# First attention scores in four row groups and four PSUM banks, tiles 10 and 11 of the FFN turned by TensorE, in a new order of work

## What is computed

```python
# 1: attention on 64 latent keys, the best 4 kept per head (16 heads of 16 columns)
Q = x @ Wq.T + bq;  V = x @ Wv.T + bv
logits = einsum('bhtd,lhd->bhtl', Q, latent) / 4
w = softmax(top_4(logits));  y = (w @ latent + V) @ Wo.T + bo
x = layernorm(x + y)
# 2: attention on 64 rows of a context (rope applied), 16 heads, folded weights
scores = q_r @ k_r.T;  ctx = softmax(scores) @ kv_rope;  x = layernorm(x + (ctx @ w_kc_kv) @ Wo.T)
# 3: FFN with ternary weights and activations rounded to 8 bits
linear_bit(x, w, g) = round_to_127(g * rmsnorm(x)) @ ternary(w).T
h = silu(linear_bit(x, w1, g1)) * linear_bit(x, w2, g2)
x = layernorm(x + linear_bit(h, w3, g3))
```

## Time and profile before

| | |
|---|---|
| median of 3 runs | 341.52 us |
| the profiled execution: its time | 342.95 us |
| its span, first to last instruction | 341.2 us |
| mean granted TensorE clock | 0.986 |
| transfers | 22.28 MB, of them 15.01 MB read from HBM |

### The profile page before, as it was taken

How to read it: one execution, slowest core, us unless ns; L and a number is a source line. 1 busy time by engine, 2 the same in 40 slices (tenths; PEclk the granted TensorE clock), 3 DMA queues, 4 the chain that set the end, 5 groups by cost and what they waited for, 6 DMA issues and landing times.

```text
span 341.2 us, 6916 instructions
## 1 busy us (share of the span) xinstructions
PE 322.0 (94%) x2245; PEld 232.6 (68%) x2264; DVE 285.6 (84%) x718; ACT 281.7 (83%) x535; POOL 249.9 (73%) x234
## 2 busy tenths in 40 slices
PE   8899999998899999999999999999999999989892
PEld 4677777766667677767777866776768767666341
DVE  2475489999499999998989999898999998798882
ACT  2476888984768778989899789899999898998883
POOL 3274757799297798989958697989489686577661
PEclk9699999999999999999999999999999999999998
DMA  7989830000000002011021102130401222210001
GB/s 214 422 325 386 281 140 0 2 1 3 0 2 1 17 1 46 2 38 41 1 46 37 28 4 46 32 63 1 48 17 32 62 35 52 55 33 16 13 22 46
DMA packets 24852, 22.28 MB, mean 65 GB/s; under 512 B 19824, under 2 KB 22256, under 8 KB 23920
## 3 DMA queue, kind: packets, MB, share of 16 engines
q1 hardware_dynamic: 24816, 21.84, 21.6%
...
HBM read 15.01 MB, written 2.10 MB: 50 GB/s over the span
## 4 chain that ended last, share of the span: by engine, by line
PE 44%; DVE 24%; issue 12%; POOL 9%; ACT 8%; DMA 2%; SPq 0%; POOLq 0%; DVEq 0%; ACTq 0%
PE small L585 6%; PE wide L550 5%; PE wide L471 3%; PE wide L483 3%; PE wide L534 3%; PE small L458 3%; DVE m L1105 3%; PE small L635 3%; DMA region_r<-in_wqkr 2%; DVE r L1170 2%; PE wide L564 2%; PE wide L609 2%; DVE ch L1236 2%; DVE m L1157 2%; PE small L506 2%
## 5 line engine op out<-in xcount | busy, mean ns | idle before, releaser
L585 PE MATMUL small<-V_sb,PT_sb 128*128 128x256 f32 x256 | 58.1, 380 | 0.3
L585 PEld LDWEIGHTS small<-V_sb,PT_sb 128*128 128x128 f32 x256 | 47.9, 190 | 8.4 <-issue 1.2
L1375 POOL TENSOR_TENSOR Ls<-Ls,m 128x1024 f32<-128x1024 f32 x16 | 31.5, 1967 | 26.1 <-DVE mask L1119 26.1
L550 PE MATMUL wide<-B_sb,x1T 128*128 128x512 f32 x192 | 49.4, 406 | 1.1 <-ACT PT_sb L866 1.0
L550 PEld LDWEIGHTS wide<-B_sb,x1T 128*128 128x128 f32 x192 | 35.2, 188 | 13.0 <-ACT PT_sb L866 2.7
L1440 POOL TENSOR_TENSOR region_c<-region_c,region_q 128x1024 f32<-128x1024 f32 (+1 forms) x17 | 32.6, 1919 | 14.5 <-DVE region_c L1229 12.0
L1105 DVE MAX8 m<-Ls 128x8 f32<-128x64 f32 x256 | 33.9, 210 | 8.9 <-ACT Ls L796 8.7
L1390 POOL TENSOR_TENSOR Ls<-Ls,mask 128x1024 f32<-128x1024 f32 x16 | 38.8, 2427 | 2.4 <-ACT Ls L809 1.8
L1413 POOL TENSOR_TENSOR P<-P,r 128x1024 f32<-128x1024 f32 x16 | 34.0, 2125 | 4.5 <-DVE r L1173 4.5
L1382 POOL TENSOR_TENSOR mask<-mask,r 128x1024 f32<-128x1024 f32 x16 | 30.4, 1902 | 8.4 <-DVE r L1128 8.4
L609 PE MATMUL wide<-tern,region_k 128*128 128x512 bf16 x111 | 28.1, 379 | 1.7 <-issue 0.6
...
## 6 DMA issues: line engine op xcount, KB each, us to landing
region_q<-in_wqx SPq DMA_DIRECT2D x1, 2048.0 KB, 17.3
region_c<-in_woTx SPq DMA_DIRECT2D x1, 2048.0 KB, 7.7
...
region_c<-in_wkcqT SPq DMA_DIRECT2D x1, 1536.0 KB, 11.8
...
```

Of the source, the lines that this page charges most:

```text
L550: mm = pe.matmul(ps_L2[:, r * 512:(r + 1) * 512], x1T[:, u, k, :], B_sb[:, s, w, k, r * 512:(r + 1) * 512], start=(u == w == k == 0), stop ...
L585: mm = pe.matmul(ps_O2[:, 0:D], PT2_sb[:, c, :], V_sb[:, c, :], start=(c == 0), stop=(c == PAIRS - 1))
L1375: pool.tensor_tensor(heads(Ls[n % 2][:]), heads(Ls[n % 2][:]), over_heads(m8[:, :, 0:1]), ALU.subtract).then_inc(g_d1, 1)
```

## The change

`L1` is cut finer: 8 products instead of 4 for a tile, each with 32 rows (2 heads) of weights and 128 columns of result, in four row groups that write four banks. These are half of each bank of `wide[1]` and `wide[2]`, so `L1` now waits for both and takes both. `lat_k` has two heads side by side instead of four and is made by one reduction and 2 products instead of 4. `copy_L1` still has two instructions of 512 columns, each now reads from the two banks of one wide tile. `TURNED` goes from 12 to 10: tiles 10 and 11 are turned by TensorE too. Several other steps move to other PSUM tiles, and the order of work is written anew on all engines.

```diff
-TURNED = 12
+TURNED = 10
-        lat_k = sb("lat_k", [P, KD, 4 * L])
+        lat_k = sb("lat_k", [P, KD, 2 * L])
+        odd_even = sb("odd_even", [P, 2])
-        ps_L1 = wide[1]
-        ps_XQT = small[1]
-        ps_HT = small[0]
+        ps_XQT = small[0]
+        ps_HT = wide[0]
-        ps_T2T = wide[2]
+        ps_T2T = wide[1]
-        ps_V = (wide[2], wide[2])
-        ps_T1 = (wide[2], wide[0])
-        ps_A = (wide[1], wide[2])
+        ps_V = (wide[2], wide[1])
+        ps_T1 = (wide[0], wide[1])
+        ps_A = (wide[0], wide[0])
-        ps_Z_last = (wide[0], wide[1])
-        ps_HT_last = (wide[0], wide[2])
+        ps_L1 = (wide[1], wide[2])
+        ps_Z_last = (wide[1], wide[2])
+        ps_HT_last = (wide[1], wide[0])
             def L1(n, *freed):
-                bank_of(*freed)
+                for k in range(0, len(freed), 2):
+                    bank_of(*freed[k:k + 2])
                 for g in range(KD):
-                    for j in range(2):
-                        mm = pe.matmul(ps_L1[:, j * 512 + g * SEQ:j * 512 + (g + 1) * SEQ],
-                                       QT[b % QRING][j * L:(j + 1) * L, g, q * P:(q + 1) * P],
-                                       lat_k[j * L:(j + 1) * L, g, :], start=True, stop=True)
+                    for j in range(4):
+                        rows = slice(32 * j, 32 * (j + 1))
+                        col = (j % 2) * 512 + g * 2 * L
+                        mm = pe.matmul(ps_L1[j // 2][:, col:col + 2 * L],
+                                       QT[b % QRING][rows, g, q * P:(q + 1) * P], lat_k[rows, g, :],
+                                       start=True, stop=True)
-            warm(9, wide[0]); Q(0); warm(4, wide[0], p_warm, 1); L1(0); T1_(0)
-            T1_(1, p_warm, 2); L1(1, a_L1, 1); Q(1, a_Q, 1); T2_(a_T1, 2); L1(2, a_L1, 2)
+            warm(9, wide[0]); Q(0); warm(4, wide[0], p_warm, 1); L1(0)
+            warm(5, wide[0], p_warm, 2); L1(1, a_L1, 1, a_L1, 1); T1_(0, p_warm, 3)
+            T1_(1, a_L1, 2); Q(1, a_Q, 1); T2_(a_T1, 1); WF(a_Q, 2); T2T(a_T1, 2)
...
             def copy_L1(n):
-                for j in range(2):
+                for half in range(2):
                     ins = act.activation(
-                        Ls[n % 2][:].rearrange("p (g j n) -> p j g n", g=KD, j=2)[:, j],
-                        ps_L1[:, j * 512:(j + 1) * 512].rearrange("p (g n) -> p g n", g=KD), ACT.Copy)
+                        Ls[n % 2][:].rearrange("p (g h j n) -> p h g j n", g=KD, h=2, j=2)[:, half],
+                        ps_L1[half][:].rearrange("p (j y g n) -> p y g j n", j=2, y=2, g=KD)[:, 0], ACT.Copy)
...
+                link(dve.tensor_reduce(odd_even[:], head_rows[:].rearrange("p e (j i) -> p i e j", i=2),
+                                       mybir.AxisListType.XY, ALU.add))
...
             def sum_2(n):
                 dve.wait_ge(a_ex2, n + 1)
+                since(dve, v_sm2, n)
```

More of the change, by code:

```diff
@@ new lines, in _ @@
+            A_(1, a_PT1, 2); WT(1, v_y1, 1); L1(3, v_bl, 1, a_C, 1); Q(3, a_Q, 3)
+            PT1(2, a_A, 2); B_(1, 0, a_L1, 4); B_(2, 0, a_L1, 4); B_(3, 0, a_PT1, 3)
+            O1(1, a_AT, 2); X1T(0, a_Q, 4); L1(4, v_bl, 3, v_bl, 2); WT(2, v_y1, 2)
+            L2(0, v_bl, 4); O1(2, a_AT, 3); X1T(1, v_xlo, 1); L1(5, a_L1, 5, a_L1, 5)
+            PT1(3, v_sub2, 1); L2(1, a_PT1, 4); C_(1, a_L1, 6); PT2(0, v_sub2, 2); S3(v_xlo, 2)
+            WT(3, v_y1, 3); X1T(2, c_mean, 2); V_(1, 0, a_C, 2); PT1(4, a_PT2, 1)
@@ new lines, in _ @@
+            V_(0, 1, a_L1, 9); O1(6, a_AT, 7); PT2(2, v_bl, 8); Z_(0, 0, None, a_V0, 2)
+            Z_(1, 0, None, v_bl, 7); L2(4, a_PT2, 3); O2(2, v_y1, 7); PT2(3, v_sub2, 5)
+            L1(9, v_g2, 1, v_g1, 1); X1T(5, v_xlo, 5); PT1(7, a_PT2, 4); O2(3, v_y2, 3)
+            L2(5, a_PT1, 8); Z_(0, 1, None, a_L1, 10); WT(7, v_y2, 4); V_(1, 2, a_L1, 10)
+            O1(7, a_AT, 8); Z_(1, 1, None, a_V1, 3); PT1(8, v_sub2, 6); O3(0, v_xlo, 6)
+            V_(0, 2, v_g1, 2); PT2(4, a_PT1, 9); WT(8, v_y1, 8); L1(10, v_g2, 2, a_V0, 3)
@@ new lines, in _ @@
+            WT(10, v_y1, 10); B_(2, 2, v_g2, 4); B_(3, 2, a_PT1, 11); Q(7, v_y3, 3)
+            V_(0, 3, v_bl, 10); L2(8, v_bl, 12); L1(12, v_bl, 11, a_V0, 4); O1(10, a_AT, 11)
+            Z_(0, 4, None, a_L1, 13); PT2(7, v_sub2, 9); O2(6, v_y1, 11)
+            Z_(1, 4, None, a_L1, 13); O2(7, v_y2, 7); V_(1, 4, v_g2, 5); PT1(11, a_PT2, 8)
+            O3(3, a_Q, 8); L1(13, a_V1, 5, v_g1, 5); X1T(9, v_y3, 4); WT(11, v_y2, 8)
+            V_(0, 4, a_L1, 14); L2(9, a_PT1, 12); Z_(0, 5, None, a_V0, 5); X1T(10, v_xlo, 10)
@@ new lines, in _ @@
+            X1T(12, v_y3, 6); B_(1, 3, a_L1, 16); Z_(1, 7, None, a_V1, 6); PT1(14, v_sub2, 12)
+            O3(6, v_xlo, 13); B_(2, 3, v_g2, 8); WT(14, v_y1, 14); B_(3, 3, a_PT1, 15)
+            V_(0, 5, v_bl, 14); O1(14, a_AT, 15); PT2(10, v_bl, 16); X1T(13, v_y3, 7)
+            Z_(0, 8, None, a_V0, 6); L2(12, a_PT2, 11); O2(10, v_y1, 15); PT2(11, v_sub2, 13)
+            Z_(1, 8, None, v_bl, 15); L2(13, a_PT2, 12); O2(11, v_y2, 11); V_(1, 6, v_g2, 9)
+            Z_(0, 9, None, v_g1, 9); O3(7, v_xlo, 14); PT1(15, v_sub2, 14)
@@ new lines, in _ @@
+            Z_(1, 11, None, a_V1, 8); PT2(14, a_hT, 1); O3(10, v_y3, 10)
+            Z_(0, 12, None, a_V0, 8); O2(14, a_qT, 3); HT(11, None, a_PT2, 15)
+            Z_(1, 12, None, v_g2, 12); XQT(13, v_y2, 15); PT2(15, a_hT, 2)
+            Z_(0, 13, None, v_g1, 13); Z_(1, 13, None, v_g2, 13); O2(15, a_qT, 4)
+            HT(12, None, a_PT2, 16); O3(11, v_y3, 11); warm(9, wide[1], v_g2, 14)
+            XQT(14, v_y2, 16); warm(3, wide[1], p_warm, 4); Z_(0, 14, None, v_g1, 14)
+            Z_(1, 14, None, p_warm, 5); O3(12, v_y3, 12); HT(13, None, a_hT, 3)
@@ L702, in _ @@
+            XQT(15, a_qT, 5); warm(2, wide[1], v_g2, 15); O3(13, v_y3, 13)
+            Z_(0, 15, 0, p_warm, 6); Z_(0, 15, 1); Z_(1, 15, 0, v_g1, 15); Z_(1, 15, 1)
+            warm(5, wide[0], a_hT, 4); HT(14, None, p_warm, 7); O3(14, v_y3, 14)
+            warm(7, wide[0], a_hT, 5); HT(15, 0, v_g1, 17); HT(15, 1, p_warm, 8)
+            warm(2, wide[2], v_g2, 17); O3(15, v_y3, 15)
         @block.scalar
@@ L1024, in _ @@
+            whole_h(13); whole_x2(15); copy_HT(13); copy_XQ(15); square_h(14); square_3(12)
+            tanh(15, 0); tanh(15, 1); whole_h(14); copy_HT(14); square_h(15); square_3(13)
+            whole_h(15, 0); whole_h(15, 1); square_3(14); copy_HT(15, 0); copy_HT(15, 1)
+            square_3(15)
         @block.vector
```

375 lines of the change are left out of this document (166 added, 209 removed).

## The result

The changed kernel takes 345.72 us (median of 4 runs, 345.24 to 346.61), the kernel before, run beside it, 342.15 us (341.06 to 342.80). The ratio is 1.0124, 95% interval 1.0103 to 1.0146: slower by 1.2%, where 335.6 us had been forecast. (1.24% are 4.2 us; the two medians by themselves differ by 3.6 us, at the lower end of the interval.) The profiled execution took 345.24 us, its span is 343.5 us.

The account below looks back on a forecast made before the run. PE was taken as the bound, DVE close behind. Start -4.3, L1 -6.2, turning +1.3 and waits +3.3 sum to -5.9 us: 335.6 us from the median 341.52, own range 333.5 to 338, whole range 331.5 to 343.0.

Parts of the forecast that it names:

- The start, -4.3 us: Before T2_: L1 of tile 1 moves ahead of T1_ and the clock stays at 2.4 GHz, saving 4.3 us.
- L1 by itself: Each tile's L1 on PE: 0.62 us instead of 1.06, saving 0.44 us a tile, bounds 0.06 and 0.49.
- WT's row: Lower bound for L1's time: WT's 16 instructions of 128 columns, four at a time, take 0.57 us.
- B_'s: Upper bound for L1's time: B_ with two groups at a time, 16 instructions in 1.00 us.
- The other 14 L1 stand on PE's full stretches: 6.2 us: L1 of tiles 2 to 15, where PE is full: 14 x 0.44 = 6.2 us saved, bounds 0.8 and 6.9.
- Turning, +1.3 us: Tiles 10 and 11 turned by PE, ahead of the last O2: two XQT and two HT add 1.3 us.
- The waits for PSUM, +3.3 us: From tile 5 on, L1 holding both wide tiles adds 0.3 us for each of 11 L1; bounds 0 and 12.
- the 7 to 10 forecast: Sign of being right: PE idles 7 to 10 us between 60 and 300 us, newly before Z_, B_ or V_.
- The end, 0: From the last tile's O2 to the end: same steps as before, put at nothing, bounds -1 and +2 us.
- That of the PSUM waits: Rival: PE waits before Z_, B_ or V_ until ACT empties four banks; 344.4 us, chance 0.16.
- The clock did fall: Rival: at the start the clock falls all the same, saving 1.0 instead of 4.3 us; 338.9 us, chance 0.15.
- The signs of being wrong: L1 near 1.0 us, clock below 0.8 after 10 us, middle PE idle over 15 us, or end over 36 us.

Follow-up runs that it names:

- e3: The changed kernel with L1 in its old form (two products of 64 rows and 256 columns), both wide tiles still held; 346.28 us, ratio 1.0137 to the kernel before.
- e15: The changed kernel with one DVE instruction moved, norm_3(2) ahead of largest_h(4); 342.88 us, ratio 1.0033 to the kernel before.
- e13: The kernel before, unchanged, profiled again; 341.05 us, span 339.3 us.
- e1: The kernel before with only the new start: L1(1) and 5 warm products ahead of T1_(0), copy_L1(1) behind copy_L1(0) on ACT; 342.34 us, ratio 1.0005.
- e5: The kernel before with only half of the products of each L1 from tile 2 on, order, tiles and waits untouched; 339.78 us, ratio 0.9948.
- e12: The kernel before with 14 of 16 maxima in max_8 on DVE from tile 2 on, PE untouched; 341.50 us, ratio 0.9990.
- e4: The changed kernel with TURNED = 12, so tiles 10 and 11 go through the transposing transfers as before; 356.43 us, ratio 1.0410.
- e14: The kernel before with TURNED = 10, so tiles 10 and 11 are turned by PE; 351.68 us, ratio 1.0302.
- e2: The kernel before with L1 as four row groups in both wide tiles, three L1 later on PE and three copies earlier on ACT; 370.63 us, ratio 1.0828.
- e7: The changed kernel's order with L1 in its old form, holding only wide[1]; 346.74 us, ratio 1.0149 to the kernel before.
- e9: The changed kernel's lists up to 110 us, then the kernel before's, with L1 in two groups from L1(9) on; 342.68 us, ratio 1.0020.
- e11: The changed kernel's lists up to 190 us, then the kernel before's, with four row groups up to L1(12); 343.08 us, ratio 1.0045.

## Why the prediction was wrong

Three steps carry it. All of the change but L1's form was put at +0.3 us (start -4.3, turning +1.3, waits +3.3); e3 measures +1.37%, 4.7 us. The form was put at -6.2 us; from e3 to e15 it is -3.6. The collision of norm_3(2), which no term holds, adds 3.1 (e15). Together that is +4.2 us by the ratios, the measured 1.24%, where -5.9 was forecast.

- **The start, -4.3 us: a failed premise.** The step took "T1_ waits for its weights until 10.13 us" and the clock of 0.58 as the kernel's, from one execution, and took the whole saving from the median too, although that execution was 1.43 us above it. In e13 the same kernel starts T2_ at 15.46 us, as early as the changed one. e1 measures the term: 0. The range had no case for it.
- **L1 by itself.** Right: 0.66 us a tile against 0.62, the price by WT's row and not by B_'s.
- **"The other 14 L1 stand on PE's full stretches: 6.2 us": a size that failed.** e5 takes the same work from PE in the old order and gets 1.8 us; in the new order it is 3.6 (e3 to e15). The step took 234 of 240 us busy for a bound. It is a high share and no bound: ACT, DVE and GpSimd hand each tile on in a fixed order, and e12 shows that DVE isn't the bound alone either.
- **Turning, +1.3 us.** Its work is there (1.8 us more busy); its price by itself was not settled (e4, e14).
- **The waits for PSUM, +3.3 us.** Right for the wrong kernel: e2 shows such waits, 13.5 us behind copy_L1 alone, in the old order; in the new one e7 against e3 shows no time. PE's idle time grew to 10.5 us in the middle, just above the 7 to 10 forecast, but hardly before Z_, B_ or V_ by ACT's copy of Ls (0.2 us before B_): X1T(9) has 1.9 us of it, L1(7) 1.5 for low_B.
- **What no term held: the new order itself.** I priced it at nothing but PSUM waits. That it costs some 4 us even without the collision is shown by e3; by which steps is not. It also put norm_3(2) close to weights_2(9), and there 0.2 us decides: with L1's old form they pass (e3, e7), with the new one they meet. From this follow 2.12 us on DVE, 1.86 us of waiting on PE, a fall of the clock and some 3 of the 4 us lost (e15). That they meet just in the version with the faster L1 is chance, not a price of four row groups.
- **The end, 0.** 310.83 to 343.5 is 32.7 us from the last O2, against 34.0 before: right, slightly better.
- **The rivals.** That of the PSUM waits gave 344.4 us, near the result by luck, as its mechanism takes no time here. The clock did fall, at 199 us and not at the start.
- **The signs of being wrong.** L1 near 1.0 us, idle time over 15 us, an end over 36 us: none came. The clock was below 0.8 after 10 us, but at 200 us and not at the start, which was meant. The list watched the terms of the sum, and the loss lay outside of them.

What stays open: e15 is still 0.33% slower than the kernel before (0.19 to 0.46%), with L1's form working in it. What eats it is the 1.37% of e3: new order, new start and turning together. In the profiles e3 has 3.7 us more busy time of PE than e13 (325.0 against 321.3, of it 1.8 turning and some from a fall of the clock at 334 us) and 2.7 us more idle time. With the cut at 110 us (e9) the mixture is 0.20% slower than the kernel before, at 190 us (e11) 0.45%; no single place was found.
